# The last addition of a rotary embedding, placed on another engine of one NeuronCore

## The reference

```
def _rope(x, positions):
    ang = positions * inv_freq
    cos, sin = jnp.cos(ang), jnp.sin(ang)
    x1, x2 = x[..., 0::2], x[..., 1::2]
    r1 = x1 * cos - x2 * sin
    r2 = x1 * sin + x2 * cos
    return jnp.stack([r1, r2], axis=-1).reshape(x.shape)

qkv = jnp.einsum('bsd,ed->bse', layernorm(x), W_qkv)     # D = 1024, 16 heads of 64, S = 2048
q, k = _rope(q), _rope(k)
scores = causal(q k^T / 8);  attn = softmax(scores);  x = x + (attn v) W_o^T
x = x + expert_ffn(layernorm(x))
```

## Time and profile before

| | |
|---|---|
| time, median of 2 runs | 5997.49 us (5981.92 to 6013.06) |
| the profiled execution | 5993.66 us, its span 5991.7 us (core 6) |
| spans of the eight cores | 5967.3 to 5991.7 us |
| mean granted TensorE clock | 0.648 to 0.650 on each core |
| busy share of the span | PE 70%, DVE 37%, ACT 27%, POOL 24% |

### The profile page before, as it was taken

The page is one execution under the profiler, slowest core; times in us unless marked ns, Lnnn a source line. Parts: engine busy times, 40 slices in busy tenths (PEclk is TensorE's granted clock), DMA queues, the critical chain, the costliest instruction groups (busy, mean ns, idle before and its releaser), DMA issues. The chain is left out here.

```text
span 5991.7 us, 47439 instructions; the slowest of 8 cores (5967.3 to 5991.7 us)
## 1 busy us (share of the span) xinstructions
PE 4165.9 (70%) x11476; PEld 1242.3 (21%) x11476; DVE 2245.6 (37%) x2561; ACT 1632.1 (27%) x1983; POOL 1416.9 (24%) x1736
## 2 busy tenths in 40 slices
PE   0066899985346799998335689999634669999843
PEld 0022222222112222223002222222201222222210
DVE  1144333334434333333434433333444443333344
ACT  0000455540000155552000035555100015555300
POOL 0018100002234610010340820000133370000033
PEclk9989555557569855556657965555756885555665
DMA  5410000001031000002021100000203100000101
GB/s 138 127 46 22 1 1 1 1 11 63 11 109 34 13 1 1 1 1 71 4 88 53 23 2 1 0 1 1 74 5 111 35 15 0 1 1 1 57 18 67
DMA packets 151776, 180.64 MB, mean 30 GB/s; under 512 B 89823, under 2 KB 110559, under 8 KB 151015
## 3 DMA queue, kind: packets, MB, share of 16 engines
q1 hardware_dynamic: 151532, 177.61, 9.7%
HBM read 133.54 MB, written 44.04 MB: 30 GB/s over the span
## 5 line engine op out<-in xcount | busy, mean ns | idle before, releaser
L633 ACT ACTIVATE PT<-pss,ecol_s 128x1024 bf16<-128x1024 f32 x1280 | 1357.5, 1111 | 1361.2 <-PE pss L605 1354.7
L571 DVE RECIPROCAL rb<-po 64x512 f32<-64x512 f32 x256 | 859.8, 3359 | 1904.6 <-PE po L561 1904.6
L605 PE MATMUL pss<-qkT 64*128 64x512 bf16 x2560 | 1198.8, 621 | 2.1 <-ACT PT L633 2.1
L539 PE MATMUL po<-PT,v 128*65 128x512 bf16 (+3 forms) x2560 | 1061.3, 569 | 1.4 <-POOL PT L650 1.0
L650 POOL TENSOR_SCALAR_AFFINE_SELECT PT<-PT 128x128 bf16<-128x128 bf16 x1024 | 275.8, 293 | 2643.7 <-ACT PT L633 2643.0
L561 PE MATMUL po<-lr,ones_s 1*64 1x512 f32 x512 | 491.2, 1060 | 241.3 <-ACT lr L554 241.3
L469 PE MATMUL psq<-u1T,wqk 128*128 128x512 bf16 x2048 | 484.1, 380 | 220.5 <-DVE t1b L482 220.5
L539 PEld LDWEIGHTS po<-PT,v 128*65 128x65 bf16 x2560 | 349.6, 162 | 822.9 <-issue 787.2
L605 PEld LDWEIGHTS pss<-qkT 64*128 64x128 bf16 x2560 | 269.0, 126 | 1070.9 <-issue 1068.8
L872 PE MATMUL psz<-t,ones_s 128*1 128x512 f32 x256 | 224.6, 1031 | 368.0 <-DVE t L861 368.0
L495 POOL TENSOR_TENSOR t2b<-qks,ropeB_s 128x512 f32<-128x512 f32 x256 | 324.6, 1268 | 659.1 <-DVE t1b L482 622.9
(11 more groups left out here) (96 smaller groups left out, 2176.6 us busy)
## 6 DMA issues: line engine op xcount, KB each, us to landing
xb<-x SPq DMA_DIRECT2D x64, 512.0 KB, 3.7
xr<-x SPq DMA_DIRECT2D x64, 512.0 KB, 3.8
out<-x2o SPq DMA_DIRECT2D x64, 512.0 KB, 2.6
wqk<-wqk_b SPq DMA_DIRECT2D x64, 256.0 KB, 3.0
cbuf_f<-wqk SPq DMA_DIRECT2D x16, 512.0 KB, 4.8
wvb<-wv_b SPq DMA_DIRECT2D x32, 256.0 KB
wob<-wo_b SPq DMA_DIRECT2D x32, 256.0 KB
wqk_b<-cbuf_b SPq DMA_DIRECT2D x16, 256.0 KB, 2.8
```

Of the source, the lines that this page charges most:

```text
L539: e.matmul(pso[i_hqb % 2][0:65, sigma:512], vsb[:, j * NH * 66 + h * 66: j * NH * 66 + h * 66 + 65], PT[:, sl4 * 512 + sigma: sl4 * 512 + ...
L571: e.reciprocal(rb[sl][:, :], posb[sl][64:128, :])
L605: e.matmul(pss[sl2][:, (jj % 2) * 512: (jj % 2) * 512 + 512], qkT[hb:hb + 64, kcol + jj * 128: kcol + (jj + 1) * 128], qkT[hb:hb + 64, qco ...
L633: e.activation(PT[:, slot0 * 512: slot0 * 512 + 1024], pss[sl2][:, :], AF.Exp, bias=self.ecol[:, 1:2], scale=0.125) \
```

## The change

The addition of `t1b` and `t2b` into `qkT` is taken out of POOL's program and recorded for DVE, directly behind the shuffle and `t1b` of its own iteration, with a wait for POOL's `t2b`. `t2b` gets a second buffer. The semaphores change their meaning: `s_qkT` now counts POOL's multiplies (and still frees `qks` for DVE, two iterations on), `s_macc` counts DVE's additions, and POOL waits for it before it writes a `t2b` buffer again, two iterations on. POOL's wait for its own multiply (`s_chg`) goes. At the head of `p2a` PE waits for the 64 additions on `s_macc`.

```diff
-                t2b = self.sb(scb, f"t2b{s}", [128, 512], F32)
+                t2b = [self.sb(scb, f"t2b{s}_{i}", [128, 512], F32)
+                       for i in range(2)]
                 psq = self.psq
                 self.qkT_base = self.s_qkT.n
+                b_add = self.s_macc.n
+                self.rope_done = (self.s_macc, b_add + NH * self.NQB)
...
-                        c1 = self.s_chg.inc()
-                        w_own = b_qkT + i if i >= 1 else 0
-
-                        def _gp(e, h=h, qb=qb, sl=i % 2, w=v_rope, c1=c1,
-                                wo=w_own):
+                        w_t2 = b_add + i - 1 if i >= 2 else 0
+
+                        def _gp(e, qb=qb, sl=i % 2, w=v_rope, wo=w_t2):
                             e.wait_ge(self.s_rope.h, w)
                             if wo:
-                                e.wait_ge(self.s_qkT.h, wo)
-                            e.tensor_mul(t2b[:, :], qks[sl][:, :],
+                                e.wait_ge(self.s_macc.h, wo)
+                            e.tensor_mul(t2b[sl][:, :], qks[sl][:, :],
                                          self.ropeB[:, qb * 512:qb * 512 + 512]) \
-                             .then_inc(self.s_chg.h, 1)
-                            e.wait_ge(self.s_chg.h, c1)
+                             .then_inc(self.s_qkT.h, 1)
+                        self.add("gpsimd", _gp)
+                        v_gp = self.s_qkT.inc()
+                        self.add("vector", lambda e, h=h, qb=qb, sl=i % 2,
+                                 w=v_gp: (
+                            e.wait_ge(self.s_qkT.h, w),
                             e.tensor_add(qkT[:, h * S + qb * 512:
                                              h * S + qb * 512 + 512],
-                                         t1b[sl][:, :], t2b[:, :]) \
-                             .then_inc(self.s_qkT.h, 1)
-                        self.add("gpsimd", _gp)
-                        self.s_qkT.inc()
+                                         t1b[sl][:, :], t2b[sl][:, :])
+                             .then_inc(self.s_macc.h, 1)))
+                        self.s_macc.inc()
...
-            self.add("tensor", lambda e, w=self.qkT_base + NH * self.NQB:
-                     e.wait_ge(self.s_qkT.h, w))
+            self.add("tensor", lambda e, rd=self.rope_done:
+                     e.wait_ge(rd[0].h, rd[1]))
```

## The result

The changed kernel takes 6150.27 us (median of 9 runs, 6146.33 to 6173.47) against 5996.41 us (8 runs), a ratio of 1.0261 with a 95% interval of 1.0241 to 1.0281. The profiled execution took 6149.7 us, its slowest core was core 4. The predicted 6155 is 5 us off.

The account below looks back on a forecast made before the run. POOL was taken to bound the stage at 2.83 us an iteration; a serial DVE and POOL chain of 3.47 us makes stages of 222.2 us, 160.6 us more over four, on 5993.7: 6155 us, range 6110 to 6196.

Parts of the forecast that it names:

- The bound before, and its length: Loop of L463 to L504: POOL's multiply and add bound it at 2.83 us an iteration, 182.1 us a stage.
- The turns: DVE's add waits for POOL's t2b, POOL's next multiply for DVE, so both alternate: 3.47 us an iteration against 2.83.
- The sum: The chain of one iteration through DVE and POOL, added term by term: 3.47 us, bounds 3.33 to 3.66.
- mask load to end of `t1b`: DVE's first part of each iteration, mask load, shuffle and t1b: 1.33 us.
- to POOL's start: Handing on from t1b's end on DVE to the start of POOL's multiply: 0.15 us.
- to DVE's start: Handing on from the end of POOL's t2b to DVE's add: 0.12 us.
- addition, to the next mask load: DVE's add of 0.68 us, less 0.08 us by which the next instruction starts before it ends.
- cycle: One iteration of the stage's loop, 64 a sequence, as a serial chain of DVE and POOL: 3.47 us.
- The total: Four stages 160.6 us longer, the rest of the kernel untouched: 6155 us, 2.7% more than before.
- The clock: Rival: TensorE's clock falls in the stage, slowing the start of attention by 28 us in all, 6183; 1 in 10.
- The gain: Rival: DVE does not stand for the add, cycle 1.95 us, stage 127 us, 5773 us; 4 in 100.

Follow-up runs that it names:

- the swapped waits: Changed kernel with POOL's two waits in the other order, the one for the t2b buffer ahead of the one for t1b: 6138.21 us, ratio 1.0238.
- addition without a wait: Changed kernel with DVE's addition reading ropeA and ropeB, so not waiting for POOL, the embedding's result left out: 5720.48 us in one execution.
- two later: Changed kernel with each addition recorded two iterations later on DVE, three buffers each of t1b and t2b, POOL's buffer wait first: 5738.28 us, ratio 0.9581.
- one later: Changed kernel with each addition recorded one iteration later on DVE, behind the next shuffle and t1b: 5764.3 us, ratio 0.9621.
- one later, waits swapped: Changed kernel with each addition one iteration later on DVE and POOL's buffer wait ahead of its wait for t1b: 5754.54 us in one execution.
- addition from PSUM: Wait-free addition kernel, but the addition reads psq and ropeB and stands between shuffle and t1b, the embedding's result left out: 5780.28 us in one execution.

## Why the prediction was right, point by point

**The bound before, and its length.** POOL's two instructions at 1.41 us each; 182.1 us a stage, four stages 728.4. Over all cores it is 727.5 to 728.6.

**The turns.** That DVE stands behind its own wait, and POOL behind DVE, was the step that decided. The timeline shows it in each cycle, and the experiments show it as the cause: without the wait 117.2 us, with the same wait two iterations later 120, with the wait in its place 223.4. The second buffer, priced at nothing, brings nothing.

**The sum.** Term by term, predicted and read from the rows of after:

| | predicted | measured |
|---|---|---|
| mask load to end of `t1b` | 1.33 | 1.30 (436.17 to 437.47) |
| to POOL's start | 0.15 | 0.20 |
| `t2b` | 1.27 | 1.27 |
| to DVE's start | 0.12 | 0.10 |
| addition, to the next mask load | 0.68 - 0.08 = 0.60 | 0.61 (0.69 reported) |
| cycle | 3.47 | 3.48 |

Two small errors cancel in part. The mask load, which went 0.03 us ahead of the shuffle when DVE came out of a wait, starts together with it when it doesn't. And the handing on to POOL is 0.05 to 0.06 us longer from the third iteration on, because of the second wait that POOL comes to late (the swapped waits take it away). The prediction took 0.15 us from the stage's first iteration, the one place of the old trace where POOL stood waiting, and that place has no second wait. That the mask load would start before the addition has ended, which no row of before showed, was taken right (0.08 us).

**The total.** Predicted were 160.6 us more in the four stages; 166 came. The total grew by 154 and not by 166, since the slowest core lay nearer to the others in the changed kernel's runs, so 6155 hit 6150 with some luck. What causes the before kernel's larger distance between slowest and median core wasn't settled. In its profiled execution the four slowest cores, 4 to 7, are those that were granted 0.81 of the clock for 43 to 48 us, and no core of the changed kernel's was; but of the kernel with one `t2b` buffer cores 4 and 5 had it for 138 and 127 us and were not among the slowest.

**The clock.** Its rival did not occur. The stands between groups of matmuls grew to 1.60 us (1.58 forecast), and the granted clock stayed at 1.00, the level of 2.4 GHz, in this stretch of the first stage and the next, and at 0.99 over the stage as a whole, against 0.97 in the earlier trace rows, whose first 18 us were granted 0.82:

```profile
500.00:525.00 25.00, 13.16 (x55) 4.98 (x56) 13.88 (x29) 0.00 (x0) 8.86 (x7) 1.00 0.10 22
```

The Trainium skill's rule (TensorE: Matmul & The Clock Gate, section "A second HAM failure mode: psum-queue depth-cycling"), by which such stands can make the clock swing, is not borne out here.

**The gain.** Its condition was named rightly as the place of the next `t1b` ahead of this addition. Its price, a cycle of 1.95 us and 5773 us, lies near the 1.93 and 5764.3 of the kernel made so, but by luck. 1.33 + 0.68 less two overlaps of 0.08 is 1.85, not 1.95, and DVE's own work takes 1.82 to 1.83 us where nothing holds it. What adds the rest in that kernel are two things that the prediction does not have: the loop through both engines, and POOL's multiply at 1.63 us beside the addition.

## What to carry to other kernels

An instruction that is moved to an idle engine takes its wait along, and an engine's busy share says nothing about where that wait will stand: write one cycle down as a chain, across the engines, in the order of each engine's program, and add it up. If a result comes back from another engine, record its use one or two iterations behind, with one buffer more than that, so that the next iteration's first half is already issued; then the second buffer has something to overlap. Judge such a stage by its own length in the trace and not by the total. A wait that is long over belongs ahead of the one that comes last; here that gave 0.06 us an iteration where the two engines took turns, and nothing where they overlapped.

## What the runs showed of the hardware

**An addition of two tiles in SBUF and POOL's multiply hold each other up.** The multiply on POOL takes 1.27 us alone, and longer the more of an addition that has already started lies beside it; the part beside is from POOL's start to the next start on DVE plus the 0.08 us by which DVE's instructions overlap:

| kernel | beside the addition | multiply | longer by |
|---|---|---|---|
| changed, taking turns | 0 | 1.27 | 0 |
| addition without a wait | 0.30 + 0.08 | 1.53 | 0.26 |
| two later | 0.37 + 0.08 | 1.59 | 0.32 |
| one later | 0.42 + 0.08 | 1.63 | 0.36 |
| one later, waits swapped | 0.48 + 0.08 | 1.69 | 0.42 |
| addition from PSUM | 0.43, or all 0.67 | 1.27 | 0 |

In each of the four kernels the multiply is longer by all of the time beside but 0.12 to 0.14 us, while the addition keeps its 0.69 to 0.70 us. So POOL stands for nearly all of it, and DVE does not notice. The Trainium skill (SBUF — State Buffer, section "Who interferes with whom") says that a DVE instruction with two inputs in SBUF contends with a GpSimd instruction that reads SBUF, and one with at most one such input doesn't; both halves agree with these rows. That it is POOL that pays holds for this order, in which the addition had started first.

The other case stands at the stage's end in the kernel of two later, where additions follow each other beside POOL's last multiply. These are the first two of the three additions in the row of 538.39 above (shortest/median/longest in ns):

```profile
L508 DVE TENSOR_TENSOR qkT<-t1b,t2b x2: 703/1240/1776, 538.4 to 539.0; 128x512 bf16<-128x512 f32 x2
```

The second starts at 539.0, with the multiply under way since 538.64, and takes 1.78 us: it ends 0.54 us after the multiply (538.64 + 1.58 = 540.22), which itself lost no more than beside one addition. So here DVE pays, 1.09 us. It is so in 29 of the 32 stages of that execution. In the other three the second addition keeps 0.70 to 0.73 us and the multiply takes 2.18. What decides between the two was not found.

**A granted clock of 0.81.** In the kernel of one later PE hardly stands, and in the profiled execution some cores of one die went at 0.81 for a part of their stages, two of them in the first two stages. Core 4, busy time by stretch (PE, weight loads, DVE, ACT, POOL, granted clock, DMA share, GB/s):

```profile
475.00:500.00 25.00, 25.00 (x96) 10.33 (x95) 22.91 (x47) 0.00 (x0) 18.07 (x13) 0.81 0.13 31
500.00:525.00 25.00, 24.73 (x104) 9.66 (x102) 24.25 (x51) 0.00 (x0) 20.19 (x13) 0.95 0.15 34
525.00:550.00 25.00, 24.46 (x105) 9.23 (x104) 24.86 (x52) 0.00 (x0) 21.20 (x13) 1.00 0.14 32
```

and the same core's timeline, with a cycle of 2.10 us and DVE standing for PE, where core 0 had 1.93 and no such stand:

```profile
472.80 0.01 DVE L486 LOAD_MASK_SELECT qks<-psq  x1 [0.17 <-PE psq L473]
...
474.90 0.01 DVE L486 LOAD_MASK_SELECT qks<-psq  x1 [0.18 <-PE psq L473]
```

The stage takes 131.6 and 132.4 us there (the first two of cores 4 and 5), not 125.2: a gain which makes PE the next bound can be given back in part by the clock.

It does not need this kernel. With one `t2b` buffer, where PE stands in each cycle, cores 4 and 5 were granted 0.81 up to 506 us in the first stage:

```profile
450.00:475.00 25.00, 16.10 (x58) 5.47 (x56) 13.98 (x31) 0.00 (x0) 8.86 (x7) 0.81 0.09 21
```

There it cost the stage nothing, as a group of 8 matmuls took 2.26 us in a cycle of 3.48. The kernel before had it too, cores 6 and 7 up to 446 us. In all three it was there ahead of the stage already, from 416 us at the latest. The profiled executions of the four other kernels in which PE stands little (without a wait, from PSUM, two later, one later with the waits swapped) show no 0.81 at all. So the stage's denser matmuls alone don't explain it, and what brings it on stays open.
